# FFN: inverse norms by logarithm and exponential from one ScalarE table, and one more head's outer product of five tiles on ScalarE instead of GpSimd

## The reference

```python
q = (h @ Wq + bq).reshape(B, S, 8, 64)            # 8 heads of 64
q = (q - mean) / sqrt(var + 1e-5) * gamma + beta  # mean, var over all tokens and heads
q0, q1 = l2norm(q[..., :32]), l2norm(q[..., 32:]) # x / max(norm, 1e-12)
s0, s1 = q0 @ l2norm(key0).T, q1 @ l2norm(key1).T # 32 scores each
ts0, ti0 = top_k(s0, 4); ts1, ti1 = top_k(s1, 4)
comb_s = ts0[..., :, None] + ts1[..., None, :]    # 16 pairs; all 16 are kept
w = softmax(comb_s)
out = sum_k up[idx] * gelu(down[idx] . h) * w     # idx = ti0 * 32 + ti1, 256 experts
```

## Time and profile before

| | |
|---|---|
| Time, median of 3 runs | 405.86 us (405.62 to 405.95) |
| Span of the profiled execution, first to last instruction | 403.8 us |
| TensorE busy in the span | 395.0 us (98%) |
| VectorE busy | 300.1 us (74%) |
| ScalarE busy | 237.8 us (59%) |
| GpSimd busy | 215.9 us (53%) |
| ACT_TABLE_LOADs of the FFN's inverse norms and exponentials | 10, of 1283 ns each |

### The profile page before, as it was taken

The page is one execution under the profiler, slowest core; times in us unless marked ns, Lnnn a source line. Parts: engine busy times, 40 slices in busy tenths (PEclk is TensorE's granted clock), DMA queues, the critical chain, the costliest instruction groups (busy, mean ns, idle before and its releaser), DMA issues.

```text
span 403.8 us, 7801 instructions
## 1 busy us (share of the span) xinstructions
PE 395.0 (98%) x2584; PEld 367.1 (91%) x2584; DVE 300.1 (74%) x1093; ACT 237.8 (59%) x519; POOL 215.9 (53%) x209
## 2 busy tenths in 40 slices
PE   8999999999999999999999999999999999999877
PEld 7878888899999999999999999999788899999766
DVE  5797768786757867476864848572986989899996
ACT  3886859454764466464545434342557977779462
POOL 1788999764385333153430300000166858989993
PEclk9999999999999999999999999999999969999999
DMA  7900213004434312233211000000100000000102
GB/s 226 310 2 1 83 55 102 8 11 128 128 89 121 118 30 59 58 84 104 65 47 30 2 0 2 1 2 2 27 1 2 0 2 2 28 28 27 41 28 67
DMA packets 19992, 21.38 MB, mean 53 GB/s; under 512 B 3180, under 2 KB 16624, under 8 KB 19952
## 3 DMA queue, kind: packets, MB, share of 16 engines
q1 hardware_dynamic: 18832, 19.96, 16.5%
q10 hardware_dynamic: 1120, 0.92, 0.7%
HBM read 18.78 MB, written 2.10 MB: 52 GB/s over the span
## 4 chain that ended last, share of the span: by engine, by line
PE 80%; POOL 12%; DVE 4%; issue 3%; DMA 1%; ACT 0%; SPq 0%; DVEq 0%; POOLq 0%; ACTq 0%
PE keep_pQ L75 11%; PE keep_pQ L76 11%; PE keep_pQ L77 11%; POOL ffn_prod L1258 9%; PE context_pA L1051 6%; PE context_pA L1053 6%; PE context_pA L1052 6%; PE context_pR L1085 6%; PE context_pR L533 3%; PE context_pA L533 3%; POOL ffn_near L1326 2%; PE ffn_pK L1807 2%; PE context_pR L75 2%; PE context_pR L77 2%; PE context_pR L76 2%
## 5 line engine op out<-in xcount | busy, mean ns | idle before, releaser
L899 DVE TENSOR_TENSOR att_pTl<-context_pR,att_pTh 128x512 fp32r<-128x512 f32 x64 | 36.9, 586 | 29.8 <-ACT att_pTh L811 29.5
L811 ACT ACTIVATE att_pTh<-context_pR 128x512 fp32r<-128x512 f32 x64 | 32.1, 514 | 40.1 <-PE context_pR L1085 40.1
L1258 POOL TENSOR_TENSOR ffn_prod<-ffn_first,ffn_near 128x1024 f32<-128x1024 f32 (+1 forms) x29 | 54.1, 1885 | 2.1 <-DVE ffn_first L1684 2.1
L851 ACT ACTIVATE att_prob<-keep_pQ,att_nmax 128x1206 f32<-128x1206 f32 x16 | 20.3, 1269 | 35.9 <-DVE att_nmax L935 35.8
L930 DVE TENSOR_REDUCE att_mx<-keep_pQ 128x1 f32<-128x402 f32 x64 | 34.5, 564 | 6.9 <-PE keep_pQ L77 6.6
L1837 PE MATMUL ffn_pT<-keep_ident,ffn_prod 128*128 128x128 f32 x240 | 30.5, 283 | 3.7 <-POOL ffn_prod L1258 3.7
L1837 PEld LDWEIGHTS ffn_pT<-keep_ident,ffn_prod 128*128 128x128 f32 x240 | 28.6, 148 | 5.8 <-DVE ffn_hT L1717 4.8
L786 POOL TENSOR_TENSOR keep_rstd<-att_ve,keep_mhalf 128x4 f32<-128x4 f32 x3 | 3.0, 1007 | 55.9 <-DVE att_ve L989 55.9
L1085 PE MATMUL context_pR<-keep_ident,att_prob 128*128 128x128 f32 (+1 forms) x208 | 31.8, 272 | 0.2 <-DVE att_pTl L899 0.2
L1051 PE MATMUL context_pA<-att_pTh,att_cNh 128*128 128x256 f32 (+1 forms) x104 | 31.0, 298 | 0.0
L1051 PE MATMUL context_pA<-att_pTh,context_cNh 128*128 128x256 f32 (+1 forms) x104 | 30.9, 297 | 0.0
(11 more groups left out here) (336 smaller groups left out, 1300.3 us busy)
## 6 DMA issues: line engine op xcount, KB each, us to landing
keep_raw<-in_ctxT SPq DMA_DIRECT2D x24, 256.0 KB, 2.7
keep_raw<-in_ctx SPq DMA_DIRECT2D x24, 256.0 KB, 3.0
out<-keep_x SPq DMA_DIRECT2D x16, 128.0 KB, 1.7
keep_x<-in_x SPq DMA_DIRECT2D x3, 512.0 KB, 9.9
gru_wout<-in_W_out SPq DMA_DIRECT2D x1, 512.0 KB, 8.7
keep_raw<-in_fWq SPq DMA_DIRECT2D x2, 256.0 KB
keep_raw<-in_ctxT SPq DMA_DIRECT2D x8, 32.5 KB, 3.1
keep_raw<-in_ctx SPq DMA_DIRECT2D x4, 65.0 KB
```

What stands on the lines that cost most here:

```text
L811: act.activation(to, bank, ACT.Copy).then_inc(bank_high, 1)
L899: dve.tensor_tensor(to, bank, half(it, 0, n)[0].bitcast(F32), ALU.subtract).then_inc(bank_free, 1)
L1258: return eng.tensor_tensor(prod[:, i % PB, a:b].rearrange("p h (i j) -> p h i j", j=KEYS), (factor if factor is not None else first[:, n % ...
```

## The change

Two edits, both in the FFN.

The inverse norm is no longer ScalarE's square root followed by VectorE's reciprocal. ScalarE takes `Ln` of `n2` and then `Exp` with scale -0.5, which gives the first guess of the inverse root directly; VectorE's Newton step stays. `Ln` and `Exp` are in one table, which is loaded before the first norms and again after the late gelus.

For tiles 4, 6, 8, 10 and 12 (`HELPED`) GpSimd's second product instruction covers 3 heads and not 4. The last head is done by ScalarE as 8 scaled copies, `head_products(j)`, placed in iteration j + 2 behind the two `leftover`s. TensorE's `sum_heads` of these tiles waits for ScalarE's part as well.

```diff
-    n2, nroot, nt, nu = (st.sb(n, [P, MOST]) for n in ("n2", "nroot", "nt", "nu"))
+    n2, nlog, ny, nt, nu = (st.sb(n, [P, MOST]) for n in ("n2", "nlog", "ny", "nt", "nu"))
...
-    ny = pB[:, 128:128 + MOST]
...
+    HELPED = range(2 * PER, LASTS - 1, PER)
...
+    def act_heads(i):
+        return SPLIT[i] if i in SPLIT else (HEADS - 1, HEADS)
+
+    def act_parts(i):
+
+        return len([j for j in (*HELPED, *SPLIT) if j <= i])
...
-                outer(pool, i, HEADS // 2, HEADS).then_inc(prod_done, 1)
+                outer(pool, i, HEADS // 2, HEADS - 1 if i in HELPED else HEADS).then_inc(prod_done, 1)
...
         def norm_roots(k):
             act.wait_ge(n2_ready, k + 1)
             m = len(BATCHES[k]) * PER * HALVES
-            act.activation(nroot[:, 0:m], n2[:, 0:m], ACT.Sqrt).then_inc(nroot_ready, 1)
+            act.activation(nlog[:, 0:m], n2[:, 0:m], ACT.Ln).then_inc(nlog_ready, 1)
+            act.wait_ge(nlog_ready, k + 1)
+            act.activation(ny[:, 0:m], nlog[:, 0:m], ACT.Exp, scale=-0.5).then_inc(nroot_ready, 1)
...
-            for h in range(*SPLIT[i]):
+            for h in range(*act_heads(i)):
...
         squared(0)
         gelu(EARLY_GELU - 1)
+        act.preload_act_table_set(LOG_EXP)
         norm_roots(0)
...
             if t == 0 and n >= 1:
                 for j in range(1 if n == 1 else i - PER, i):
                     leftover(j)
+                for j in range(i - PER, i):
+                    if j in HELPED:
+                        head_products(j)
             if i == PER * BATCHES[-1][-1] - 2 * PER:
                 for m in range(EARLY_GELU, ES):
                     late_gelu(m)
+                act.preload_act_table_set(LOG_EXP)
...
             dve.wait_ge(nroot_ready, k + 1)
-            a = note(dve.reciprocal(yy, nroot[:, 0:m]))
-            yield
-            need(a)
             a = note(dve.scalar_tensor_tensor(out=t, in0=n2[:, 0:m], scalar=-0.5, in1=yy, op0=ALU.mult,
                                               op1=ALU.mult))
...
+            if i in SPLIT or i in HELPED:
+                pe.wait_ge(part_act, act_parts(i))
             if i in SPLIT:
-                pe.wait_ge(part_act, i - LASTS + 2)
                 pe.wait_ge(part_dve, i - LASTS + 2)
```

More of the change, by code:

```diff
@@ L25 @@
 NORM_EPS = 1e-12
+LOG_EXP = "natural_log_exp_and_others"
 HEADS, QD = 8, 64
@@ L1201, in stage_ffn @@
     mv_ready, avg_mm, bn_ready = st.sem("mv_ready"), st.sem("avg_mm"), st.sem("bn_ready")
-    sq_ready, sq_pool, norm_mm, n2_ready, nroot_ready, ninv_ready = (
-        st.sem(n) for n in ("sq_ready", "sq_pool", "norm_mm", "n2_ready", "nroot_ready", "ninv_ready"))
+    sq_ready, sq_pool, norm_mm, n2_ready, nlog_ready, nroot_ready, ninv_ready = (
+        st.sem(n) for n in ("sq_ready", "sq_pool", "norm_mm", "n2_ready", "nlog_ready", "nroot_ready", "ninv_ready"))
     q_ready_dve, q_ready_pool, q_ready_act = (st.sem(n) for n in ("q_ready_dve", "q_ready_pool", "q_ready_act"))
@@ L1848, in sum_last @@
                 if h == SPLIT[i][0]:
-                    pe.wait_ge(part_act, 3)
+                    pe.wait_ge(part_act, act_parts(i))
                 if h == SPLIT[i][1]:
```

## The result

| | time, median | runs | span of the profiled execution |
|---|---|---|---|
| before | 405.90 us | 4, 405.62 to 406.03 | 403.8 us |
| after | 412.02 us | 4, 411.91 to 413.13 | 411.2 us |

The changed kernel is slower: 1.0167 of before, 95% interval 1.0145 to 1.0188. The forecast was 407.2 us with a range up to 408.6: the sign was right, the size was not, and the measured time lies 3.4 us above the range. The delay that I had worked out is in the trace, and beside it a larger one that I had given no price. The profiled execution of the kernel after is the slowest of the four, 413.13 us, and the one of before an ordinary one; so the traces lie 7.4 us apart and the medians 6.1.

What follows compares the result with a forecast made beforehand. The prediction took TensorE as the bound from 340 to 375 us and VectorE for the last 20 us. A 1.36 us delay at tile 12, 0.06 absorbed, gave 405.86 + 1.3 = 407.2 us, range 405.4 to 408.6.

Steps and rivals of the forecast that it cites:

- The delay that I had worked out: Tile 8's copies on ScalarE delay tile 12's exponentials: VectorE's MAX8 1.36 us late, net +1.30 us at the end; chance 0.68.
- the part on the reciprocal: Five reciprocals leave VectorE; in the last batch, near 367, this saves 0.35 us, bounds 0.1 and 0.55.
- all given back at the waits for TensorE's `norms`: Ahead of 366 us the earlier batches save VectorE 0.1 to 0.6 us each, lost again waiting for TensorE.
- TensorE's times up to 375 as before: Sign of a right forecast: TensorE's start times up to 375 us unchanged, the `norms` at 364.41 among them.
- TensorE goes at its own pace: FFN, 340 to 375 us: TensorE busy 35.00 of 35.00 us, so faster GpSimd or VectorE gains nothing unless TensorE waits.
- A fall behind an idle gap: Rival, chance 0.08: the clock halves behind a 2.5 us gap before tile 11's sum, two sums cost 3.4 us; 409.5 us.
- Gaps of 1.56 and 1.73 us did nothing in this trace: Argument against the clock falling in a new gap: TensorE's idle times at 376.72 and 385.84 brought no fall.
- the table loads and reciprocals give little at the end: Eight table loads of 1.28 us go from ScalarE, but the copy at 367.49 waits for TensorE: nothing gained; reciprocal 0.35 us.
- the wait is ended by `ffn_e`: Sign of a right forecast: VectorE idle about 1.7 us, until `ffn_e`, before its MAX8 at 375.6.
- the gap ahead of tile 11's sum: TensorE's idle time before tile 11's sum, at about 386.6, grows from 1.73 to 2.5 us.
- GpSimd is not the bound: Against the rival that GpSimd bounds the kernel and 5 x 0.41 = 2.05 us come off: 403.8 us, chance 0.04.
- a clock that dips less: Rival, chance 0.08: the half-clock dip at 328 to 330 goes or moves, TensorE 1.7 to 3.3 us earlier; 404.7 us.

Runs made afterwards that it cites:

- e1: The changed kernel with the first guess `ny` written back to PSUM and not to SBUF: 405.43 us, ratio 1.001 to before.
- e2: The kernel before with one edit, the reciprocal writing `ny` to SBUF and not to PSUM: 413.97 us, ratio 1.0208.
- e7: The changed kernel with `ny` left in SBUF and the other Newton operands (`n2`, `nt`, `nu`) moved to PSUM: 406.62 us, ratio 1.0034.
- e5: The changed kernel with `ny` in PSUM and no heads moved, so logarithm and exponential alone: 405.53 us, ratio 0.9991.
- e6: The changed kernel with `ny` in PSUM and tile 8's heads all left on GpSimd (4, 6, 10, 12 helped): 404.15 us, ratio 0.9981.
- e4: The changed kernel with no heads moved, so logarithm and exponential alone, `ny` still in SBUF: 414.07 us, ratio 1.0206.
- e8: The changed kernel with `ny` in PSUM and only tiles 10 and 12 helped: 403.37 us, ratio 0.9958.
- e9: The changed kernel with `ny` in SBUF only for the batch of groups 4 and 5, PSUM for the others: 410.98 us, ratio 1.0147.
- e10: The changed kernel with `ny` in SBUF only for the batch of groups 2 and 3, PSUM for the others: 407.25 us, ratio 1.0055.
- e3: The changed kernel with root and reciprocal as before, `ny` in PSUM and no preloads, so the heads alone: 408.18 us, ratio 1.0092.

## Why the prediction was wrong

**The step that failed** is the part on the reciprocal. It priced the reciprocal that goes (0.35 us) and took the Newton steps behind it as unchanged, and what the earlier batches do as "all given back at the waits for TensorE's `norms`". But the diff moves `ny` from `pB`, a PSUM tile, to SBUF, and with it all three steps of each batch to two SBUF inputs. That edit got no price. The rows to see it by were there: `near` and the products keep GpSimd busy 32.43 of 35 us, so a step that must wait for the end of one of its instructions would mostly have to. By the earlier trace rows such an instruction lasts 0.87, 1.89 or 1.48 us, three steps a batch: 0 to 5.7 us of delay a batch was the bound to put down. The runs give 0.2 us a step against up to 1.84 (e1 against e2 and the kernel after), 7.4 us more in fifteen steps.

The Trainium skill ("SBUF — State Buffer", section "Who interferes with whom") has this as a rule: a VectorE instruction with two SBUF inputs contends with a GpSimd instruction that reads SBUF, one with at most one SBUF input and outside the two-port modes doesn't, and the loser stands still until the other's instruction is over. This trace agrees, 0.21 us at 329.42 beside 1.83 at 330.56, and e7 agrees on the other half. It bore on a line of the diff that I had read only as a change of name and size.

**TensorE's times up to 375 as before**: wrong, and the text says what it would mean: that the stretch isn't TensorE's, or that the clock came out differently. Both happened. "TensorE goes at its own pace" from 340 to 375 was true of before, but I read it as robustness. TensorE was full because ScalarE's squares came just in time (354.31 to 355.63, the `norms` at 354.91); a delay of 2 us on VectorE reached it through `ffn_s`, ScalarE's queue and `ffn_sq`. Slack of the links behind a full engine doesn't show in its busy share.

**The clock.** A fall behind an idle gap had a chance of 0.08 and was placed at tile 11's sum. It happened, but at 334 and 358, behind 2.14 and 1.84 us of idle time; the second fall cost 3.5 us, close to the 2 x 1.68 = 3.4 that had been worked out for the other place, which is chance. "Gaps of 1.56 and 1.73 us did nothing in this trace" was true and didn't carry over.

**Right**, by e1, e5 and e6: the table loads and reciprocals give little at the end (e5, 0.9991; 0.4 us at granted clock 0.992, though 1.2 at 1.00); the copies of tile 8 delay tile 12's exponentials and VectorE's MAX8, 1.36 us forecast and 1.35 in e1. That the changed kernel shows 1.36 as well (7.58 - 6.22) is luck: its held step makes 1.0 of it, and e4 has the same delay without a copy; the wait is ended by `ffn_e` (1.49 us in e1 against a forecast 1.7; 0.35 in the changed kernel, where VectorE comes late itself); the gap ahead of tile 11's sum is 2.56 in e1 against 2.5 (in the changed kernel 1.66, at 392.90); GpSimd is not the bound. In the measured time the heads cost less than 1.3 us: e1 stands at 1.001 with an interval that holds both 0 and 1.3 us, e7 at 1.0034, which is 1.4 us. In e1's trace the step from the last `norms` to the last sum is 1.30 us longer than before (35.18 - 33.88), the forecast's net 1.30.

**Left open.** Most runs of the kernels without the hold fall into two groups some 1.5 to 2.7 us apart (e1: 404.6 to 405.7 and 407.4 to 407.9). The profiles of e6 and e8 have the clock at 1.00 throughout, that of before falls to 0.50 at 328; that the two groups are this fall present or absent is likely, since a profile with it stands 3.3 us behind one without at group 4 and 2.5 us behind at group 5, and e5's groups lie 2.5 us apart (405.63 and 403.17). But no experiment switched it, and the groups of before lie only 1.6 us apart (406.02 and 404.42). The forecast's rival of a clock that dips less is thus something that comes and goes between executions of one kernel and not a result of the change.

## What to carry to other kernels

For every edit that moves a tile between PSUM and SBUF, list the VectorE instructions that read it and ask what GpSimd runs beside them: an instruction of 0.2 us with two SBUF inputs can last as long as GpSimd's whole instruction, and one input in PSUM removes this. When an engine is full, ask how late its inputs are allowed to come before calling a delay elsewhere free. Price idle time of TensorE twice, once for itself and once for the clock behind it, and take the absence of a fall behind one gap as no promise for the next.

## What the runs showed of the hardware

- VectorE's step of 128x64 with two SBUF inputs took 0.21 us alone and 0.53 (e2) to 1.84 us beside a GpSimd instruction that reads SBUF, ending with it; with one input in PSUM it took 0.18 to 0.23 us in all five batches, whichever of the inputs it was (e1, e7).
- The granted clock fell to 0.50 behind idle times of 2.14 and 1.84 us (after, 333 and 358), 2.21 us (e9, 355), 2.55 us (e10, 387), 1.19 and 1.23 us (e2 and e4, 359), 0.75 us (e3, 354) and 0.65 us (e7, 336; e2 and e4, 340), and stayed at 1.00 behind 0.62 and 0.64 (e9, e3), 1.56 and 1.73 (before), 2.47 (after, 384), 2.56 (e1), and 2.86 and 2.91 us (e2 and e4, 386). The length of the gap alone doesn't decide it in these runs.
- The fall to 0.50 at 326 to 334 us, where TensorE had no idle time, is in the profiles of before, e1, e2, e4, e5 and e10, and not in those of the changed kernel, e3 and e6 to e9. Where it is, the `norms` of group 4 come 3.3 us later behind those of group 2, and those of group 5 2.5 us later, than in e6, e8 and e9.
